# A head-pair epilogue's denominator copies moved from ScalarE to VectorE and put first, and a scratch write moved from the ScalarE to the GpSimd DMA queue

## What is computed

```python
c_kv = h @ W_dkv + b_dkv;  c_q = h @ W_dq + b_dq
k = concat(c_kv @ W_uk, rotary(h @ W_kr));  v = c_kv @ W_uv
q = concat(c_q @ W_uq,  rotary(c_q @ W_qr))
attn = softmax(q @ k.T / 8)
x = layernorm(h + (attn @ v) @ W_o + b_o)
y = x @ int4_quantised(W_ffn) + bias + (x @ a) @ b
out = layernorm(x + y)
```

## Time and profile before

| | us |
|---|---|
| median of 2 runs | 3214.79 |
| the profiled execution | 3213.51 |
| its span on the slowest core (core 5) | 3212.0 |
| spans of the 8 cores | 3197.2 to 3212.0 |
| busy: PE, ACT, DVE, POOL | 2507.5, 2194.8, 1168.3, 210.4 |
| chain that ended last: PE, DVE, ACT, issue, DMA | 55%, 13%, 11%, 10%, 9% |

### The profile page before, as it was taken

How to read it: one execution, slowest core, us unless ns; L and a number is a source line. 1 busy time by engine, 2 the same in 40 slices (tenths; PEclk the granted TensorE clock), 3 DMA queues, 4 the chain that set the end, 5 groups by cost and what they waited for, 6 DMA issues and landing times.

```text
span 3212.0 us, 40217 instructions; the slowest of 8 cores (3197.2 to 3212.0 us)
## 1 busy us (share of the span) xinstructions
PE 2507.5 (78%) x10584; PEld 788.5 (25%) x10584; DVE 1168.3 (36%) x1494; ACT 2194.8 (68%) x2481; POOL 210.4 (7%) x356
## 2 busy tenths in 40 slices
PE   0555759999788988898888978987899788988733
PEld 0222312222222222222222222222222222222211
DVE  3267211212433244324342443244423443334244
ACT  0233339999678976797679867986788678977600
POOL 3000000000000000000000000000000000000000
PEclk9766669999899998999999989998999899999966
DMA  5432230001212111201220121112121212121121
GB/s 93 120 95 95 86 79 19 25 14 37 71 52 70 35 63 54 76 25 48 72 76 29 45 81 52 53 42 72 55 60 44 69 48 62 39 73 56 54 89 39
DMA packets 90051, 190.27 MB, mean 59 GB/s; under 512 B 18643, under 2 KB 50644, under 8 KB 89588
## 3 DMA queue, kind: packets, MB, share of 16 engines
q1 hardware_dynamic: 47812, 86.48, 9.5%
q0 software_dynamic: 23600, 59.27, 6.7%
q10 hardware_dynamic: 18432, 41.95, 3.3%
HBM read 144.65 MB, written 51.64 MB: 61 GB/s over the span
## 4 chain that ended last, share of the span: by engine, by line
PE 55%; DVE 13%; ACT 11%; issue 10%; DMA 9%; SPq 1%; DVEq 0%; ACTq 0%; POOL 0%; POOLq 0%
PE PS L234 53%; ACT Psb L246 8%; DVE tA L251 3%; DVE bcast_sb L277 3%; PE PS L240 2%; ACT bcast_sb L246 2%; DMA h<-h 2%; DMA bcast_sb<-rden 1%; DMA rotq_scr<-c0s_sb 1%; DVE h L251 1%; DMA wbuf<-W_dq 1%; DVE Qsb L257 1%; DMA h<-x_scr 1%; DMA rden<-bcast_sb 1%; DVE Psb L257 1%
## 5 line engine op out<-in xcount | busy, mean ns | idle before, releaser
L246 ACT ACTIVATE Psb<-PS 128x1024 bf16<-128x1024 f32 x2048 | 1981.1, 1042 | 486.7 <-PE PS L234 442.1
L234 PE MATMUL PS<-Psb,Vsb 128*65 128x512 bf16 x4096 | 1331.0, 408 | 114.0 <-ACT bcast_sb L246 96.2
L234 PE MATMUL PS<-Qsb,Ksb 64*128 64x512 bf16 x4096 | 830.9, 399 | 118.0 <-ACT Psb L246 109.7
L234 PEld LDWEIGHTS PS<-Qsb,Ksb 64*128 64x128 bf16 x4096 | 221.8, 93 | 982.8 <-issue 980.0
L234 PEld LDWEIGHTS PS<-Psb,Vsb 128*65 128x65 bf16 x4096 | 294.3, 112 | 613.7 <-issue 613.7
L277 DVE RECIPROCAL bcast_sb<-bcast_sb 128x512 f32<-128x512 f32 x64 | 214.4, 3349 | 254.9 <-DMA bcast_sb<-rden 254.9
L251 DVE TENSOR_TENSOR tA<-PS,h 128x512 f32<-128x512 f32 x128 | 88.4, 691 | 585.7 <-PE PS L234 577.0
L240 PE MATMUL PS<-ident_sb,h 128*128 128x128 f32 x512 | 106.1, 366 | 192.6 <-DMA h<-h 118.4
L273 DVE CAST oun_sb<-PS 64x512 bf16<-64x512 f32 x128 | 87.3, 682 | 422.3 <-PE PS L234 420.2
L234 PE MATMUL PS<-wbuf,osb 128*128 128x512 bf16 x512 | 169.9, 419 | 48.7 <-DVE tA L251 32.6
L227 POOL DMA_DIRECT2D rden<-bcast_sb x128 | 63.1, 497 | 1967.9 <-ACT bcast_sb L246 1967.9
(11 more groups left out here) (83 smaller groups left out, 1085.6 us busy)
## 6 DMA issues: line engine op xcount, KB each, us to landing
h<-h SPq DMA_DIRECT2D x64, 512.0 KB, 3.9
wbuf<-wo_p POOLq DMA_DIRECT2D x32, 512.0 KB, 6.0
bcast_sb<-rden POOLq DMA_DIRECT2D x128, 128.0 KB, 2.8
x_scr<-tA ACTq DMA_DIRECT2D x32, 512.0 KB, 2.8
wbuf<-wf_p POOLq DMA_DIRECT2D x32, 512.0 KB, 6.5
h<-x_scr SPq DMA_DIRECT2D x32, 512.0 KB, 3.9
out<-tA ACTq DMA_DIRECT2D x32, 512.0 KB, 2.7
o_dram<-oun_sb ACTq DMA_DIRECT2D x64, 128.0 KB, 1.7
```

What stands on the lines that cost most here:

```text
L234: e.matmul(o, l, r, start=s1, stop=s2, tile_position=t, skip_group_check=k)),
L246: e.activation(o, i, f, scale=sc, bias=b)),
```

## The change

In `ep_start` the two denominator copies become DVE copies and are issued first, ahead of the two copies of the output rows. `dnev` and the wait of the `rden` write are counted on `sDV` instead of `sAC`. The write of `x1_scr` is issued on the POOL queue instead of the ACT queue. Nothing else is touched.

```diff
         def ep_start(PIDX2):
+            c1 = cp(bcast_sb[0:1, 0:512], PS[64:65, 2048:2560],
+                    waits=[("sPE", denb[lastG])] +
+                          ([("sDV", bcf_[PIDX2 - 1])] if PIDX2 > 0 else []))
+            c2 = cp(bcast_sb[32:33, 0:512], PS[64:65, 2560:3072])
+            dnev[PIDX2] = c2["sDV"]
             cp(oun_sb[0:64, op_:op_ + 512], PS[0:64, 2048:2560],
-               waits=[("sPE", denb[lastG])] +
-                     ([("qOD", norm_[PIDX2 - 2])] if PIDX2 > 1 else []))
+               waits=[("qOD", norm_[PIDX2 - 2])] if PIDX2 > 1 else [])
             e = cp(oun_sb[64:128, op_:op_ + 512], PS[0:64, 2560:3072])
             oune[PIDX2] = e["sDV"]
-            c1 = act(bcast_sb[0:1, 0:512], PS[64:65, 2048:2560], AF.Copy,
-                     waits=[("sPE", denb[lastG])] +
-                           ([("sDV", bcf_[PIDX2 - 1])] if PIDX2 > 0 else []))
-            c2 = act(bcast_sb[32:33, 0:512], PS[64:65, 2560:3072], AF.Copy)
-            dnev[PIDX2] = c2["sAC"]
-            return e["sDV"], c2["sAC"]
+            return e["sDV"], c2["sDV"]
 ...
-                        sem="qBC", waits=[("sAC", c2_dv)] +
+                        sem="qBC", waits=[("sDV", c2_dv)] +
 ...
-                w += [("sDV", oune[PIDX - 1]), ("sAC", dnev[PIDX - 1])]
+                w += [("sDV", oune[PIDX - 1]), ("sDV", dnev[PIDX - 1])]
 ...
-                xw = dma("scalar", x1_scr[128 * sub:128 * (sub + 1), :], tA[:, :],
+                xw = dma("gpsimd", x1_scr[128 * sub:128 * (sub + 1), :], tA[:, :],
```

## The result

| | before | after |
|---|---|---|
| median of all executions | 3223.2 us (10) | 3293.4 us (11) |
| lowest to highest | 3206.3 to 3319.5 us | 3280.9 to 3335.7 us |
| profiled execution | 3213.5 us | 3294.2 us |
| span of its slowest core | 3212.0 us (core 5) | 3292.6 us (core 7) |
| granted clock of the eight cores | 0.888 to 0.891 | 0.868 to 0.875 |

The ratio after to before is 1.0216, 95% interval 1.0182 to 1.0251. The forecast of 3287 us is 6 us off. Whether each of its terms was right is another question.

What follows compares the result with a forecast made beforehand. PE and ACT waiting for each other, at head-pair boundaries and the scratch write, was taken as the bound. 71 + 24 - 25 + 3 = +73 us on 3213.5 us gave 3287 us, range 3243 to 3318.

Steps and rivals of the forecast that it cites:

- Step 1: Head-pair boundaries: four DVE copies in a row, PE restarting 3.08 us behind the first copy's start; +71 us.
- Rival E: Boundaries: denominator copies run at the rate of SBUF rows, 0.42 us each; total 3245 us, chance 0.10.
- rival F: Boundaries: ACT is the bound, so its 1.21 us less per boundary shortens each pair; total 3112 us, chance 0.03.
- ACT's freed time buys nothing: Boundaries: ACT's freed 1.21 us per pair gains nothing, since its next scores stand behind the stopped matmul.
- Step 2: Behind boundary restarts: longer PE stops are followed by half clock more often; +24 us, bounds 0 and 50.
- 17 more stretches x 1.4: Behind boundary restarts: some 17 more half-clock stretches at 1.4 us each, giving +24 us.
- Step 3: Scratch write on POOL: seven stops go (-24.6), their half clock too (-10), late write gives 9 back; -25 us.
- Step 4: Last tail: DVE waits for the uncovered scratch write three times, 1 us more each; +3 us.

Runs made afterwards that it cites:

- e3: The kernel after with DVE's four copies in the other order, output rows first and denominators last; 1.0230 times the kernel before.
- e5: The kernel after with the scores of group 3 computed four times ahead of the stopped matmul, three of them repeated work; 0.9891 times the kernel before.
- e2: The kernel before with only the scratch write moved from the ACT queue to the POOL queue; 0.9945 times the kernel before.
- e4: The kernel after with the scores of group 3 computed once, ahead of the stopped matmul instead of behind it; 0.9990 times the kernel before.
- e9: The kernel after with the two denominator copies made twice, six DVE copies per boundary; 1.0554 times the kernel before.

## Why the prediction was right, and where it was not

**Step 1, four copies on DVE: right.** A copy takes 0.686 us (taken: 0.68), the restart comes 3.1 us behind the first copy in all 63 boundaries (3.08), the stops grew by 73.5 us (71). Rival E's copies at 0.42 us and rival F's earlier restart did not happen. What the Trainium skill, VectorE: DVE Perf Modes, section "Why PSUM operands drop a tier", says of an fp32 operand in PSUM agrees with the 686 ns. Missed was what the step sets free: the sentence that ACT's freed time buys nothing and that the reciprocal is hidden anyway. PE's waits for ACT's weights fell by 27 us with the copies alone. e3 leaves little to the order of the copies: with the output rows first three of the seven stops are back, 4.6 us together. That a PE slower behind the boundary gives DVE's chain of the norm time to catch up would fit, but the clock can't be the whole of it: in e5, with half clock behind 12 boundaries only, ACT's wait is back in three of the seven, at 0.6 to 1.5 us. The cause stays open.

**Step 2, the clock: the right count, the wrong size.** Forecast were about 50 boundaries below full clock, found were 53. The failed term is the price: "17 more stretches x 1.4" took a stretch to be as long after a 2.93 us stop as after a 1.75 us one. Its rows showed only the short kind; now 30 of 63 restarts have half clock for 5 us at least, where 2 had. The 138 us of additional half-clock time at e5's 0.34 are +47 us, and PE's busy time grew by 60.3 us, where steps 2 and 3 together had +24 - 10 = +14. The price per microsecond was not too low: the two pairs with a granted clock of 0.95 over some 33.7 us have 3.4 us of half clock each and cost 1.33 and 2.08 us, 0.39 and 0.62 per microsecond, somewhat more than e5's 0.34.

**Step 3, the scratch write: right in kind, too large.** The seven stops went, 25.4 us together (7 x 3.52 took two of 3.9 us for 3.52), and the write is late by 3.62 to 5.57 us of DVE's time. From DVE's end to its restart it takes 0.56 + 3.07 = 3.63 us; on ACT the issue started 0.08 us behind DVE and the last tail's wait shows 2.73 us to the restart, so 0.8 us more, where 1 was taken; 0.48 us of it is that the issue starts later. But PE gave back 24 us in e2, some 3 each with all that is put down to `tA`, where 9 us, 1.3 each, were forecast. With the clock's 7 us e2 should be -27 + 24 - 7 = -10 us, and it is -18, with an interval of 6 us either way. Forecast for the step were -25.

**Step 4, the last tail: right.** DVE's three waits there are 3.61, 3.58 and 3.55 us, before 2.81, 2.95 and 2.97: +2 us (forecast +3). The estimate of 3.2 us for this write from the Trainium skill, DMA: Bandwidth & Descriptors, section "Anatomy of one DMA — SWDGE (gpsimd) path", stands beside a measured 3.07 us from issue to DVE's restart.

**The sum.** Put together with measured terms: +73.5 stops, -52 for ACT's weights, +15 for DVE's `tA` (45.8 to 61.2 us), -5 for the reload of `h` (22.5 to 17.4 us), -6 for its first load (118.4 to 112.5 us) and -5 in small items make the +20.3 us of PE's idle time; with the +60.3 us of its busy time that is the +80.6 us of the profiled executions. The medians differ by +70. The prediction's +73 holds because its misses cancel, and that is luck: the clock cost PE 46 us more than forecast, and PE's waits for ACT fell by 27 us more, with smaller items on the same side. The last step of its addition is off by one: 3286.5 and 1.3 make 3288, not 3287, and nothing hangs on it.

## What to carry to other kernels

At a point where two engines empty an accumulator side by side and a third waits for the later of them, moving the work to one engine costs the sum, whatever share of the span that engine is idle; make the shared part shorter (one 1x1024 copy for two of 1x512) or put work of the waiting engine ahead of its stop. A stop of PE has a second price in the clock behind it, and in these kernels it grew with the stop's length as well as with the count of stops, so measure how long the half-clock stretches are and not only how many; PE's busy time at an equal count of matmuls shows what they cost, and half clock within a stop costs nothing. A DMA issue whose data isn't ready blocks the engine that issues it; a queue without a compute stream takes that stop away, but the next writer of the same buffer then becomes the one that waits.

## What the runs showed of the hardware that was not expected

- Half-clock stretches lengthen with the stop before them: behind stops of 1.77 us in the mean 34 of 63 restarts are below full clock and 2 are at 0.50 for all of 5 us; behind 2.93 us it is 53 and 30; behind 4.36 us all 63 are below. The stretches that touch a boundary last 3.6, 5.4 and 6.3 us in the mean; with the longest stops they begin during the stop at 54 restarts, so that only 19 of the 63 are at 0.50 for all of the 5 us behind it.
- Scores computed four times instead of once, in time in which PE would have stood still, make the kernel 32 us faster (e5 against e4).
- Of e9's half clock 107 us lie within the 63 stops and lengthen nothing: at 90 us more half-clock time than after, PE's busy time grew by 14 us.
- PE goes on 0.15 us behind DVE's copy of one row out of PSUM and 0.25 us behind one of 64 rows, though both copies take 0.69 us.
- A DMA issue on POOL started 0.56 us behind DVE's last scaling, one on ACT 0.08 us, and took 0.57 us of the engine instead of 0.33 us.
